# A fused two-layer block on one core: half of each feed-forward moved into the next batch's feature steps

## The reference, cut to what matters

```
xn = layernorm(x)
# s: linear attention with random Fourier features, then a feed-forward
x2 = layernorm(xn) * ln1_g + ln1_b
q, k, v = x2 @ wq + bq, x2 @ wk + bk, x2 @ wv + bv      # 16 heads of 16
feature(y) = concat(cos(y @ proj / 4), sin(y @ proj / 4)) / sqrt(128)   # 256 per head
kv = feature(k).T @ v;  a = feature(q) @ kv              # per batch and head
s = xn + a @ wo + bo
s = s + relu(layernorm(s) * ln2_g + ln2_b @ w1 + b1) @ w2 + b2     # hidden width 1024
# g: channel mixing of xn with the token before it
r = sigmoid(xr @ W_r);  kk = relu(xk @ W_k) ** 2;  g = silu(r * (kk @ W_v))
x = x + s * g
xn1 = layernorm(x)                                       # goes on to the second layer
logits = xn1 @ gate_W + gate_b                           # for its experts
```

## Time and profile before

| | |
|---|---|
| runs | 2255.49, 2257.26, 2257.49 us |
| profiled execution | 2251.99 us, span 2250.2 us |
| busy over the span | PE 1924.1 (86%), PEld 1050.7, DVE 1661.8 (74%), ACT 1266.2 (56%), POOL 1223.7 (54%) |
| first layer | to about 894 us of the span |
| one batch, output projection to output projection | 212.5, 213.5, 213.0 us |
| one batch's feature steps, first turn to output projection | 112.9 us (third batch) |

### The profile page before, as it was taken

How to read it: one execution, slowest core, us unless ns; L and a number is a source line. 1 busy time by engine, 2 the same in 40 slices (tenths; PEclk the granted TensorE clock), 3 DMA queues, 4 the chain that set the end, 5 groups by cost and what they waited for, 6 DMA issues and landing times. The chain is left out here.

```text
span 2250.2 us, 25260 instructions
## 1 busy us (share of the span) xinstructions
PE 1924.1 (86%) x7956; PEld 1050.7 (47%) x7956; DVE 1661.8 (74%) x2173; ACT 1266.2 (56%) x1685; POOL 1223.7 (54%) x651
## 2 busy tenths in 40 slices
PE   5799889988996998888989998899886667998996
PEld 3335534643464364333324333443332224887885
DVE  3973688278727833699999999999989996322787
ACT  3873585268527832566664666556653343664774
POOL 3601541072108010288888899989986775222576
PEclk9899899989998999999999999999998999999998
DMA  7510551065006312788889898998889995223453
GB/s 197 113 38 0 156 125 19 1 189 111 1 33 173 76 38 66 108 296 288 284 294 311 292 299 263 320 320 273 287 258 377 346 313 194 98 100 103 128 159 109
DMA packets 177316, 402.60 MB, mean 179 GB/s; under 512 B 48174, under 2 KB 77104, under 8 KB 176034
## 3 DMA queue, kind: packets, MB, share of 16 engines
q1 hardware_dynamic: 165154, 371.09, 53.3%
q0 software_dynamic: 12032, 29.90, 4.6%
HBM read 356.30 MB, written 45.51 MB: 179 GB/s over the span
## 5 line engine op out<-in xcount | busy, mean ns | idle before, releaser
L1230 POOL TENSOR_TENSOR late<-late,rows 128x1024 f32<-128x1024 f32 x256 | 602.7, 2363 | 143.3 <-DVE late L1710 140.1
L1881 PE MATMUL m_Q<-late,ident_m 128*128 128x512 f32 x1024 | 525.2, 645 | 151.5 <-POOL late L1230 114.4
L1710 DVE TENSOR_TENSOR_SCAN late<-m_Q,late 128x1024 f32<-128x1024 f32 x256 | 586.3, 2290 | 38.8 <-ACT m_Q L1416 10.3
L1416 ACT ACTIVATE m_Q<-late,acol 128x1024 f32<-128x1024 f32 x256 | 286.1, 1117 | 362.6 <-DVE late L1710 361.0
L1881 PEld LDWEIGHTS m_Q<-late,ident_m 128*128 128x128 f32 x1024 | 194.3, 202 | 449.9 <-POOL late L1230 263.5
L1703 DVE TENSOR_TENSOR late<-m_Q,rows 128x1024 f32<-128x1024 f32 x256 | 307.1, 1200 | 13.4 <-DMA rows<-bc_s 13.3
L492 DVE SCALAR_TENSOR_TENSOR early<-early,work 128x1024 f32<-128x1024 f32 x128 | 155.9, 1218 | 33.1 <-ACT early L628 30.8
L1944 PE MATMUL m_Q<-late 128*128 128x128 f32 x1248 | 159.7, 282 | 8.8 <-DVE m_so L1738 0.8
L1944 PEld LDWEIGHTS m_Q<-late 128*128 128x128 f32 x1248 | 147.7, 194 | 36.5 <-issue 35.2
L313 POOL TENSOR_TENSOR qkh<-early,qkh 128x1024 bf16<-128x1024 f32 x12 | 25.5, 2127 | 247.6 <-ACT qkh L596 247.6
L636 ACT ACTIVATE early<-early 128x1024 f32<-128x1024 f32 x128 | 134.8, 1053 | 42.1 <-DVE early L497 40.8
(11 more groups left out here) (234 smaller groups left out, 3330.0 us busy)
## 6 DMA issues: line engine op xcount, KB each, us to landing
rows<-bc_s SPq DMA_DIRECT2D x512, 512.0 KB, 5.8
rows<-st_s SPq DMA_DIRECT2D x64, 384.0 KB, 5.5
st_s<-qkh SPq DMA_DIRECT2D x16, 768.0 KB, 6.3
r_s<-late SPq DMA_DIRECT2D x39, 256.0 KB, 2.0
rows<-st_s SPq DMA_DIRECT2D x64, 128.0 KB, 6.4
xin<-in_x SPq DMA_DIRECT2D x4, 1024.0 KB, 8.8
xres<-in_x SPq DMA_DIRECT2D x4, 1024.0 KB, 5.8
mx_s<-s SPq DMA_DIRECT2D x4, 1024.0 KB, 4.5
```

The costliest lines, as they stand in the source:

```text
L1230: nc.gpsimd.tensor_tensor(pr[:, n % NH, :], h[:, n % NH, :], cb[:, n % NCB, :], ALU.mult).then_inc(pr_ok, 1)
L1416: A(dA[:, :], dt[:, (b * KI + m) % 2, :], ACT.Exp, scale=acol[:, m, i % NS:i % NS + 1]).then_inc(dA_ok, 1)
L1710: v_.tensor_tensor_scan(h[:, n % NH, :], dA[:, :], dB[:, n % 2, :], 0.0, ALU.mult, ALU.add).then_inc(h_ok, 1)
L1881: ins = mm(half(Y, c), ident[:, :], half(pr[:, n % NH, :], c), start=False, stop=(n % NS == NS - 1), skip_group_check=True)
```

## The change

The second half of each feed-forward but the last batch's (tokens 512 to 1023) is taken out of the tail and done in the next batch's steps: its four hidden jobs in steps 0 to 7 and its second matrix, as four jobs of 128 tokens, in steps 8 to 15, one piece a step (`BEHIND`). ACT's ReLU stands in the even steps, after the whole turns of the next step and before the sines of its own. DVE adds the four results in steps 9, 11, 13 and 15, and the gate, the residual and the normalisation of that half follow in steps 16 to 22; the transposes for the next layer and the logits move to steps 24 to 30. The mixing layer's jobs move to steps 16 to 23, first `kk`, then `r`. Within a step PE now does the sums ahead of these jobs. In the tail the next input's transposes come between the hidden jobs and `w2` of the first half. The query and key parts get four buffers of their own outside `qkh`, the gate moves from `v` to `kr`, and q and v change places in the projections. ACT's tanh moves behind the copies of the value product. SP's stores of a batch's sums, norms and turned norms and the load of the next input move into the next batch's steps. The query steps are as before.

```diff
-AMID = {13: ("r", 0), 17: ("r", 1), 20: ("kk", 0), 26: ("kk", 1)}
-TAKEN = {15: ("r", 0), 19: ("r", 1), 22: ("kk", 0), 28: ("kk", 1)}
-PREVIOUS = {2: ("xn", 0), 4: ("xn", 1), 7: ("gl",), 12: ("gate",)}
+AMID = {16: ("kk", 0), 18: ("r", 0), 20: ("r", 1), 22: ("kk", 1)}
+TAKEN = {18: ("kk", 0), 20: ("r", 0), 22: ("r", 1), 24: ("kk", 1)}
+BEHIND = {0: ("h", 1, 0), 2: ("h", 1, 1), 4: ("h", 1, 2), 6: ("h", 1, 3), 8: ("w2", 1, 0), 10: ("w2", 1, 1), 12: ("w2", 1, 2), 14: ("w2", 1, 3)}
+ADDED = {9: 0, 11: 1, 13: 2, 15: 3}
+PREVIOUS = {24: ("xn", 0), 26: ("xn", 1), 28: ("gl",), 30: ("gate",)}
...
             seq += body(b)
             if b + 1 < B:
-                seq += [(b + 1, j) for j in PRE]
+                seq += [(b + 1, j) for j in TURN_IN] + [(b, ("w2", 0))] + [(b + 1, j) for j in PRE]
...
                 def batch(b, last):
 
                     unit_in(b, 2)
+                    unit_in(b, 3)
+                    if b == 0:
+                        next_input(1)
+                    unit_in(b, 4)
+                    unit_in(b, 5)
+                    if b:
+                        sums_out(b - 1)
+                    unit_in(b, 6)
+                    if b:
+                        norms_out(b - 1)
+                    unit_in(b, 7)
                     if b:
                         turned_out(b - 1)
...
+                        if not last:
+                            next_input(b + 1)
...
+                def behind(b, s):
+
+                    if s in ADDED:
+                        add_out(b, ADDED[s])
+                    if s == 16:
+                        link(4)
+                        dv.wait_ge(s1_ok, b * 7 + 7)
+                        add_half(b, 1)
+                    elif s == 18:
+                        dv.wait_ge(x1_ok, b + 1)
+                        statistics(v_, s1, range(4, TB))
+                    elif s == 19:
+                        variances(v_, link, fresh=4)
+                    elif s == 20:
+                        square_roots(v_, link)
+                    elif s in (21, 22):
+                        normalise(v_, xh, s1, xh_ok, tiles=range(4 * (s - 21), 4 * (s - 21) + 4))
...
                         if s + AHEAD in ACT_ROUNDS:
                             whole_turns(s + AHEAD)
+                        if b and s in BEHIND and BEHIND[s][0] == "h":
+                            hidden(b - 1, *BEHIND[s][1:])
                         ac.wait_ge(ra_ok, b * 32 + s + 1)
...
-                    for i in range(2):
-                        ac.wait_ge(r_ok, b * 2 + i + 1)
-                        A(four(v, i), four(xh, i), ACT.Tanh, scale=0.5).then_inc(th_ok, 1)
                     for i in range(2):
                         wait_full(ac, b, "vv", i)
                         A(xr[:, i, :], slot(b, "vv", i)[:, :], ACT.Identity).then_inc(vv_ok, 1)
+                    ac.wait_ge(kact_ok, b * KD + KD)
+                    for i in range(2):
+                        ac.wait_ge(r_ok, b * 2 + i + 1)
+                        A(four(gt, i), four(v, i), ACT.Tanh, scale=0.5).then_inc(th_ok, 1)
...
                             key_sums(u)
                         if u >= 16:
                             attend(u - 16).then_inc(feat_used, 1)
+                        if s in AMID:
+                            besides(s, False)
+                        elif s - 1 in AMID:
+                            besides(s - 1, True)
+                        if b and s in BEHIND:
+                            behind(b - 1, BEHIND[s], (0,))
+                        elif b and s - 1 in BEHIND:
+                            behind(b - 1, BEHIND[s - 1], (1,))
...
+                    for q in range(MF // 2):
+                        hidden(b, ("h", 0, q))
+                    if not last:
+                        turned_in(b + 1)
+                    pe.wait_ge(h_ok, b * MF + MF // 2)
+                    by_token(b, ("w2", 0), lambda k, t: qkh[:, k, t * P:(t + 1) * P], w2, MF)
+                    if last:
+                        for job in BEHIND.values():
+                            behind(b, job)
```

More of the change, by code:

```diff
@@ L360, in _, with statistics @@
                         before_features(b + 1)
-            LN_LINKS = 2 * TB + 1 + 3 + 9
-            IN_LINKS = LN_LINKS + 1
-            DVE_LINKS = IN_LINKS + 2 * LN_LINKS + 2
-            def layer_norm_stats(v_, link, src, ready=None, between=None, twice=False):
-                for t in range(TB):
+            def statistics(v_, src, tiles, ready=None):
+                for t in tiles:
                     if ready:
@@ L399, in layer_norm_stats, with normalise @@
                     link(1)
-            def normalise(v_, dst, src, ok, second=False):
-                for t in range(TB):
+            def normalise(v_, dst, src, ok, second=False, tiles=range(TB)):
+                for t in tiles:
                     v_.tensor_scalar(dst[:, t, :], src[:, t, :], mv[:, t, 0:1], rs[:, 1, TB * second + t:TB * second + t + 1],
@@ L526, in batch @@
                     dv.wait_ge(sb_ok, b + 1)
-                    for c in range(NC_):
-                        wait_full(dv, b, "w2", c)
-                        v_.tensor_tensor(four(s1, c), slot(b, "w2", c)[:, :], four(s1, c), ALU.add).then_inc(s1_ok, 1)
-                    dv.wait_ge(s1_ok, b * 4 + 4)
-                    for i in range(2):
-                        dv.wait_ge(g_ok, b * 2 + i + 1)
-                        v_.tensor_tensor(four(s1, i), four(s1, i), four(v, i), ALU.mult).then_inc(dve, 1)
@@ L607, in before_features, with hidden @@
                     middle(1)
-                    values(0)
                     high(2)
                     middle(2)
-                    values(1)
+                    values(0)
                     high(3)
                     middle(3)
+                    values(1)
                 def normed(b, c):
-                    copy_transposed(b, "xn", c, lambda k: kr[:, k, c * CH:(c + 1) * CH], xnT_ok)
+                    copy_transposed(b, "xn", c, lambda k: xinT[:, k, c * CH:(c + 1) * CH], xnT_ok)
+                def hidden(b, c, q):
+                    wait_full(ac, b, "h", c, q)
+                    if c and not q:
+                        wait_full(ac, b, "w2", 0)
+                    for j in range(2):
+                        i = A(qkh[:, 2 * q + j, :], slot(b, "h", c, q)[:, j * CH:(j + 1) * CH], ACT.Relu,
+                              bias=b1c[:, 2 * q + j:2 * q + j + 1])
+                    i.then_inc(h_ok, 1)
                 def logits(b):
```

323 lines of the change are left out of this document (181 added, 142 removed).

## The result

The changed kernel takes 2197.3 us (median of four runs, 2194.57 to 2205.68) beside 2256.38 for the kernel before (2254.64 to 2257.49): a ratio of 0.9743, interval 0.9725 to 0.9762, so 59 less; forecast were 50 less and 2207. Every ratio in this document is to the kernel before, run again beside the version measured (medians 2253.79 to 2256.82), so differences in us between versions can be off by some 3.

A forecast was written before the change was run, and what follows sets the result against it. TensorE was taken as full in the tail, with idle time in the key steps. Per period 72.4 (tail, projections) + 124 (features) = 196.4 instead of 213.0, in all 50 less: 2207 us, range 2178 to 2246.

The forecast's parts named there:

- Tail and projections: Output projection to first key step: 72.4 a batch instead of 100.6, including 2.0 charged for the tanh.
- The first key turn: First key step's wait for operands out of DRAM, 0.20 before: costed at nothing, one us kept either way.
- Features: The 32 feature steps of a batch: 113.0 + 0.8 + 4 + 3 + 3 = 124, against 112.9 before.
- The waits of the mixing jobs: Steps 16 to 23: VectorE over by 2 and jobs waiting for it to empty slots, 4 in all.
- The 3 for collisions: Steps 16 to 23: VectorE, nearly full, colliding with GpSimd, 3 added to the features.
- The sum: Period 196.4 instead of 213.0, three times; with last tanh and first batch's steps, 50 less: 2207.
- The ring: Slower rival: three PSUM slots make feature steps with a job take 4.9; features 146, kernel 2275; chance 0.12.
- VectorE as the bound: Rival in the feature steps: doubled collisions, job waits of 10 not 4; features 132, kernel 2231; chance 0.17.
- The clock: Rival: key steps stay at a granted clock of 0.81; features 136.6, kernel 2245; chance 0.08.
- Everything packs: Faster rival: TensorE's 113.0 plus 3 at the end, tanh hidden; period 186.4, kernel 2175; chance 0.15 for under 2192.
- The rule on the clock: Activity releases TensorE's slow state, so the filled key steps run at the upper level, 2.4 GHz.
- The rule on GpSimd's port: GpSimd late by 4 would hold the moved multiply and add at step 16: 4 a batch, 2219.

The follow-up runs named there:

- the tanh and the three whole turns together: Changed kernel with both tanh ahead of the value copies and the whole turns of steps 17, 20 and 22 on ScalarE: 2182.47 us, ratio 0.9681.
- the run without the mixture: Changed kernel with the second product and the sum of GpSimd's mixture in the key steps cut to 8 elements: 2198.54 us, ratio 0.9755.

## Why the prediction was right, step by step

**Bound and place: right.** TensorE was full in the tail and had room in the key steps; the two runs with the half left in the tail show that the move is the gain (68 and 74) and that all other edits together are not. The window that the prediction reads as the first sixteen steps ends 4.7 behind the first query turn; TensorE's idle time in it, 16.8, is the same by either cut (62.57 less 45.77, 57.85 less 41.05), so nothing in the sum hangs on it.

**Tail and projections: 72.4 forecast; 75.28, 71.11 and 71.12 measured.** The half and its wait of 1.36 went, and the transposes cover ScalarE's last ReLU. The tanh were charged 2.0 and cost 1.34 in the second batch's tail (1.59 in place of the 0.25 of the earlier trace rows). The stretch with the first batch's tail is 4.2 longer than the next: 1.4 by the longer wait with the table load in it, 2.8 by the clock. One charge had been taken for all batches; over three it came out, by two errors of opposite sign.

**The first key turn: right**, it waits for nothing out of DRAM.

**Features: 124 forecast; 119.8, 119.05 and 120.4 measured.** This is the mis-sized term. The work of 113.0 (TensorE was busy 112.5) and the start of 0.8 (0.91) hold. The waits of the mixing jobs, 4 forecast, are 2.34 and 1.12. The 3 for collisions are not paid in the third batch: VectorE did lose 7.0 by them (18.1 less 16 times 0.69), but TensorE idled 1.64 in all of its key steps, 0.91 of it the start. The 3 at the end are 1.0 (0.19 and 0.80).

**The sum: 50 forecast, 57.4 in the profiled executions.** Features are 12.8 shorter than forecast over the three batches; against it, the first batch's steps gained nothing and not 2, the stretch behind the last output projection is 3.0 longer and not 2 (1.34 of waiting and 1.70 of slow products), and the second layer 1.7. That leaves 8 for a difference of 7.4; the tails and rounding are the rest. The other 2 or so between 2207 and 2197.3 is the allowance between profiled execution and median: 5.3 added, 2.7 found in the changed kernel. That part of the number has nothing to do with the change.

**The rivals.** *The ring* is out as a slower case: 3.31 a key step, not 4.7. A floor is there all the same, lower than feared: 45.65 for the sixteen key steps with nothing moved in, where the sines pace TensorE, and 50 with ReLUs and adds but half of the products. So TensorE is the bound of the key steps by a small margin (51.4 of 53.0, with ScalarE at 46.5 and VectorE at 45.8), and what took 14 off it gained 3. That ScalarE and VectorE together set those 50 is argued from their busy time; which of them, or the three slots, or the collisions, stays open. *VectorE as the bound* was right in kind for the query steps, where relieving it gained 9, and wrong in size: the jobs' waits are 3.5 a batch and not 10. *The clock* was wrong in the key steps (1.00), but a low mean clock (0.83, 0.89) came up where it had not been looked for, behind the new wait. *Everything packs* (2175) came close to what the tanh and the three whole turns together give, 2182.

**The rule on the clock** (the Trainium skill, "TensorE: Matmul & The Clock Gate", What's actually happening: activity releases the throttle). The runs agree: 0.89 in the key steps of the same kernel with the half left in the tail, 1.00 with it moved in. With half of the products out, the third batch's key steps stayed at 1.00 with TensorE busy 39.5 of 50.06, and the query steps behind them fell to 0.95. **The rule on GpSimd's port** would have cost 4 a batch if GpSimd were late by 4; its last addition in the third batch's steps ends at 474.04, ahead of the first query turn at 476.12, and the moved multiply and add take 1.22 each (479.62 and 480.87), so the trace shows no such cost.

## What to carry to other kernels

Look for the stage where the bounding engine is alone and the one where it has gaps, and move whole pieces from the first to the second; the price is what the gaps' own pace leaves over (here 4.9 for 27.8), not the pieces' time. Place a moved piece behind the work that is ready in the engine's order, since ahead of it the same piece cost 16. Before relieving the full engine further, look at the next two: here they were busy within 6 of it over 53, and halving the moved products gained no more than 2 of 2197.

## What the runs showed of the hardware that was not expected

- A wait of TensorE can cost twice. Behind 3.02 of idle the hidden layer's products took 16.77 in place of 14.00 (clock 0.83), behind 1.58 in the last batch 15.70 (0.89), but behind 1.59 in the second batch 14.00 (1.00). Over the eight versions with these waits, the products behind 3.0 were slow each time (15.47 to 16.79), and those behind 1.6 in five of 24 cases (15.70 each: three times in the fourth batch, twice in the third). In the kernel before and the three versions with a wait of 0.25 they took 14.00 in all 16 cases. What tells the five from the other 19 is open; it is not the place in the kernel, since the same batch is slow in one version and not in the next.
- ScalarE's first tanh brings a table load of 1.28. With the tanh first it stands in the gap ahead of the output projection (151.39) and the hidden layer's wait is 0.24; the new order put it on the path.
- An absolute value of VectorE over 128x1024 takes 0.69 alone. Begun beside a GpSimd addition it ended some 0.55 behind that addition: 4.38 in the run without the mixture, 2.21 in the changed kernel (472.38 to 474.59, the addition to 474.04). Beside a GpSimd product by a scalar it took 0.69 in some places and up to 1.58 in others; what tells these apart is open. The Trainium skill ("GPSIMD Engine Reference", Specifications) names a shared interface with VectorE, and the trace agrees that the two collide; how much it costs differed with GpSimd's instruction.
